# Turning the normalised x by a DMA transpose instead of on TensorE, in a gated cross-attention block

## The reference

```
x = x + tanh(g_xattn) * xattn(layernorm(x), ctx, ctx)      # 16 heads of 16
    q = layernorm(x) @ Wq.T + bq ; k = ctx @ Wk.T + bk ; v = ctx @ Wv.T + bv
    out = softmax(q k.T / 4) v @ Wo.T + bo
x = x + tanh(g_ffn) * ffn(layernorm(x))                    # 4-bit weights, 16-bit activations,
                                                           # a global maximum between the stages
```

## Time and profile before

| | |
|---|---|
| median of three runs | 587.03 us |
| the profiled execution's own time | 588.25 us |
| its span | 586.4 us |
| PE busy | 544.4 us (93%) |
| DVE busy | 483.0 us (82%) |
| ACT busy | 435.1 us (74%) |
| POOL busy | 191.8 us (33%) |

### The profile page before, as it was taken

How to read it: one execution, slowest core, us unless ns; L and a number is a source line. 1 busy time by engine, 2 the same in 40 slices (tenths; PEclk the granted TensorE clock), 3 DMA queues, 4 the chain that set the end, 5 groups by cost and what they waited for, 6 DMA issues and landing times. The chain is left out here.

```text
span 586.4 us, 12288 instructions
## 1 busy us (share of the span) xinstructions
PE 544.4 (93%) x4614; PEld 317.1 (54%) x4614; DVE 483.0 (82%) x818; ACT 435.1 (74%) x633; POOL 191.8 (33%) x298
## 2 busy tenths in 40 slices
PE   7779999999999998998787999999999899989998
PEld 2435555565556555664464544444444344458887
DVE  5687889999999999998556899979888799954532
ACT  2327888888888887887853454469999998889960
POOL 3412356776767697753551000000000000010000
PEclk9868999999999999999997999999999999999999
DMA  7322344546435453333220000000000000013443
GB/s 242 98 85 97 123 132 136 158 143 184 149 87 156 152 166 115 120 115 102 68 84 35 1 1 0 1 0 1 1 1 0 1 0 1 0 73 109 147 141 108
DMA packets 41472, 48.90 MB, mean 83 GB/s; under 512 B 9302, under 2 KB 29190, under 8 KB 41414
## 3 DMA queue, kind: packets, MB, share of 16 engines
q1 hardware_dynamic: 39430, 43.14, 23.6%
q0 software_dynamic: 1408, 4.46, 2.5%
q10 hardware_dynamic: 576, 0.52, 0.3%
HBM read 24.25 MB, written 8.63 MB: 56 GB/s over the span
## 5 line engine op out<-in xcount | busy, mean ns | idle before, releaser
L924 DVE TENSOR_REDUCE negm<-s_ps 128x2 bf16<-128x512 f32 x256 | 163.5, 684 | 16.6 <-PE s_ps L529 15.9
L732 ACT ACTIVATE pt<-st_ps 128x512 f32<-128x512 f32 x256 | 138.2, 594 | 40.6 <-PE st_ps L546 40.0
L1270 PE MATMUL pairs<-xq,wut 128*128 128x512 f16 x576 | 124.7, 379 | 2.7 <-ACT lnall L1464 1.6
L1270 PEld LDWEIGHTS pairs<-xq,wut 128*128 128x128 f16 x576 | 56.2, 98 | 71.1 <-issue 2.3
L529 PE MATMUL s_ps<-kst,qst 63*128 63x256 f16 x512 | 66.9, 282 | 16.6 <-DVE negm L924 13.7
L456 PE MATMUL pv_ps<-pt,vt 128*32 128x256 f32 x1024 | 68.5, 385 | 1.5 <-ACT ot L659 0.7
L1784 POOL PARTITION_ALL_REDUCE vmax<-vmax x5 | 1.8, 355 | 193.3 <-DVE vmax L1577 119.4
L1270 PE MATMUL pairs<-xq,wgt 128*128 128x512 f16 x276 | 60.5, 379 | 0.0
L546 PE MATMUL st_ps<-qst,kst 64*128 64x256 f16 x512 | 56.4, 272 | 1.7 <-ACT pt L732 1.7
L529 PEld LDWEIGHTS s_ps<-kst,qst 63*128 63x128 f16 x512 | 20.6, 94 | 54.7 <-DVE negm L924 39.7
L1376 PE MATMUL pairs<-wdt,h 128*128 128x256 f16 x384 | 47.2, 273 | 2.9 <-DVE h L1739 2.4
(11 more groups left out here) (229 smaller groups left out, 1036.7 us busy)
## 6 DMA issues: line engine op xcount, KB each, us to landing
qst<-qk SPq DMA_DIRECT2D x47, 128.0 KB, 2.1
kst<-qk SPq DMA_DIRECT2D x45, 128.0 KB, 2.1
xt<-in_x SPq DMA_DIRECT2D x16, 256.0 KB, 4.4
ct<-in_ctx SPq DMA_DIRECT2D x16, 256.0 KB, 2.9
xr<-in_x SPq DMA_DIRECT2D x16, 256.0 KB, 3.9
out<-y SPq DMA_DIRECT2D x16, 256.0 KB, 3.6
lnall<-out POOLq DMA_DIRECT2D x8, 512.0 KB, 4.3
recb<-rec_dram SPq DMA_DIRECT2D x15, 256.0 KB
```

The costliest lines, as they stand in the source:

```text
L732: nc.scalar.activation(pt[:, (j // 2) % 2, j % 2, :, r], st_ps[u % 3][:], ACT.Exp, scale=1.0 / (WS * WS * HD ** 0.5)).then_inc(exp_done, 1)
L924: nc.vector.tensor_reduce(negm[:, b % 2, :, lo], s_ps[r][:], AX.X, ALU.max, negate=True).then_inc(max_done, 1)
L1270: mm = nc.tensor.matmul(ps[:, p, k, :], w[:, a, dt, f * P:(f + 1) * P], xq[:, b, c, dt, :], start=n == 0, stop=n == len(terms) - 1)
```

## The change

For all batches but the first:

- the four transposes on TensorE (slot 6), ScalarE's copy of the bank and VectorE's subtraction (slot 7) are gone;
- ScalarE copies `xn` as it lies to f16 `xtok[:, 0]` at offset XH = -22 (slot 2), GpSimd subtracts and writes `xtok[:, 1]` at XL = -21 (slot 3);
- SyncE issues at XDMA = -19 (slot 5, between `stack_k` and `load_tops(b, 0)`) one DMA transpose of both halves, 256 KB, from `xtok` to `xtr`;
- the q projection (slot 1) waits for it (`x_turned`) and reads `xtr` in two runs of 128 columns;
- GpSimd's `normalise` waits for the copy and the subtraction of the last batch instead of TensorE;
- the two spare banks have six users, each with a fixed bank, and the waits are changed to match.

The first batch is still turned by TensorE, now in `st_ps[1]`.

```
+    XH, XL, XDMA = -22, -21, -19
-        xh = sb("xh", [P, 2, S], F16)
-        xl = sb("xl", [P, 2, S], F16)
+        xtok = sb("xtok", [P, 2, KT * D], F16)
+        xtr = sb("xtr", [P, 2, KT, 2, P], F16)
...
-            return misc[(7 * (g // PAIRS) + (0, 1, 1, 2, 3, 4, 5, 6)[g % PAIRS]) % 2]
+            return misc[{TOP1 % PAIRS: 0, Q % PAIRS: 1, K % PAIRS: 0, TOP0 % PAIRS: 1, V % PAIRS: 0, PROJ % PAIRS: 1}[g % PAIRS]]
...   # SyncE, behind stack_k and ahead of load_tops(b, 0)
+                if (b := batch(g, XDMA)) is not None and b:
+                    sp.wait_ge(xl_done, b + 1)
+                    sp.wait_ge(xh_done, b + 1)
+                    sp.wait_ge(q_done, b)
+                    sp.dma_start_transpose(xtr[:].rearrange("p i t u q -> p (i t u) q"),
+                                           xtok[:].rearrange("p i c -> p (i c)")).then_inc(x_turned, 16)
...   # TensorE, project_out
-                pe.wait_ge(v_taken, before(g, V))
-                pe.wait_ge(top_done[1], before(g, TOP1))
+                pe.wait_ge(top_done[0], before(g, TOP0))
...   # TensorE, Q
-                    pe.wait_ge(v_taken, before(g, V))
+                    pe.wait_ge(top_done[0], before(g, TOP0))
                     pe.wait_ge(xl_done, b + 1)
-                    project(bank(g), "q", xh, xl, q_done)
+                    if b:
+                        pe.wait_ge(x_turned, 16 * b)
+                    project(bank(g), "q", lambda k: xtr[:, 0, :, k, :], lambda k: xtr[:, 1, :, k, :], q_done)
...   # TensorE, TURN, now for the first batch alone
-                if (b := batch(g, TURN)) is not None:
-                    pe.wait_ge(top_done[0], before(g, TOP0))
-                    pe.wait_ge(ql_done, before(g, Q))
-                    pe.wait_ge(xl_done, b)
-                    pe.wait_ge(xn_ready, b + 1)
+                if g == TURN:
+                    pe.wait_ge(xn_ready, 1)
...   # ScalarE
-                if (b := batch(g, -17)) is not None:
-                    act.wait_ge(xt_done, b + 1)
-                    act.wait_ge(q_done, b)
-                    nc.scalar.copy(xh[:], bank(PAIRS * b + TURN)[:]).then_inc(xh_done, 1)
+                if (b := batch(g, XH)) is not None and b:
+                    act.wait_ge(xn_ready, b + 1)
+                    act.wait_ge(x_turned, 16 * (b - 1))
+                    nc.scalar.copy(xtok[:, 0], xn[:].rearrange("p t d -> p (t d)")).then_inc(xh_done, 1)
...   # VectorE
-                if (b := batch(g, -17)) is not None:
-                    dve.wait_ge(xh_done, b + 1)
-                    nc.vector.tensor_tensor(xl[:], bank(PAIRS * b + TURN)[:], xh[:], ALU.subtract).then_inc(xl_done, 1)
...   # GpSimd, normalise and behind it
-                    pool.wait_ge(xt_done, b)
+                    if b == 1:
+                        pool.wait_ge(xt_done, 1)
+                    else:
+                        pool.wait_ge(xh_done, b)
+                        pool.wait_ge(xl_done, b)
+                if (b := batch(g, XL)) is not None and b:
+                    pool.wait_ge(xh_done, b + 1)
+                    pool.wait_ge(x_turned, 16 * (b - 1))
+                    nc.gpsimd.tensor_tensor(xtok[:, 1], xn[:].rearrange("p t d -> p (t d)"), xtok[:, 0], ALU.subtract
+                                            ).then_inc(xl_done, 1)
```

More of the change, by code:

```diff
@@ L152, in attention, with two_halves @@
         recb_ps = s_ps[1][:].rearrange("p a b -> p (a b)")
-        last_ps = (misc[1][:, 0], st_ps[2][:, 0])
+        last_ps = (misc[0][:, 0], st_ps[2][:, 0])
         recx = wi[:, 0:4 * S].bitcast(F32)
-        ahl, all_ = (xh, ch), (xl, cl)
+        def two_halves(i):
+            return xtr[:, i].rearrange("p t u q -> p (t u q)").rearrange("p (u s) -> p u s", u=2)
+        ahl, all_ = (two_halves(0), ch[:]), (two_halves(1), cl[:])
         ident_zeroed = sem("ident_zeroed")
@@ L201, in attention @@
         xt_done = sem("xt_done")
+        x_turned = sem("x_turned")
         xh_done = sem("xh_done")
@@ L423, in project @@
                 for e in range(2):
-                    mm = split_product(to[:, e, :], lambda k: wh[nm][:, k, e * P:(e + 1) * P],
-                                       lambda k: wl[nm][:, k, e * P:(e + 1) * P],
-                                       lambda k: xh_[:, k, :], lambda k: xl_[:, k, :])
+                    o = to[:, e, :] if nm == "k" else to[:, e, :].rearrange("p (t q) -> p t q", t=KT)
+                    mm = split_product(o, lambda k: wh[nm][:, k, e * P:(e + 1) * P],
+                                       lambda k: wl[nm][:, k, e * P:(e + 1) * P], xh_, xl_)
                 mm.then_inc(done, 1)
@@ L514, in _ @@
             pe.wait_ge(cl_done, 1)
-            project(st_ps[0], "k", ch, cl, k_done)
+            project(st_ps[0], "k", lambda k: ch[:, k, :], lambda k: cl[:, k, :], k_done)
             spare_products(4)
@@ L576, in _ @@
                     pe.wait_ge(xl_done, b + 1)
-                    project(bank(g), "q", xh, xl, q_done)
+                    if b:
+                        pe.wait_ge(x_turned, 16 * b)
+                    project(bank(g), "q", lambda k: xtr[:, 0, :, k, :], lambda k: xtr[:, 1, :, k, :], q_done)
                 if (b := batch(g, K)) is not None and b:
                     pe.wait_ge(top_done[1], before(g, TOP1))
-                    pe.wait_ge(xl_done, before(g, TURN))
+                    pe.wait_ge(v_taken, before(g, V))
                     pe.wait_ge(kl_done, b)
                     pe.wait_ge(cl_done, b + 1)
-                    project(bank(g), "k", ch, cl, k_done)
+                    project(bank(g), "k", lambda k: ch[:, k, :], lambda k: cl[:, k, :], k_done)
                 if g == -6:
@@ L619, in _ @@
                 if (b := batch(g, TOP1)) is not None:
-                    pe.wait_ge(xl_done, before(g, TURN))
-                    pe.wait_ge(top_done[0], before(g, TOP0))
+                    pe.wait_ge(v_taken, before(g, V))
+                    pe.wait_ge(kl_done, before(g, K))
                     pe.wait_ge(max_done, UNITS * b + UNITS)
@@ L676, in high_last @@
                 act.wait_ge(v_done, NB)
-                nc.scalar.copy(ahl[v][:], at[:, 1 - v]).then_inc(ah_last, 1)
+                nc.scalar.copy(ahl[v], at[:, 1 - v]).then_inc(ah_last, 1)
             def high_of(b):
@@ L713, in _ @@
                     high(1, bank(PAIRS * b + K), kh_done)
-                if (b := batch(g, -17)) is not None:
-                    act.wait_ge(xt_done, b + 1)
-                    act.wait_ge(q_done, b)
-                    nc.scalar.copy(xh[:], bank(PAIRS * b + TURN)[:]).then_inc(xh_done, 1)
[L718 to L724, removed]
+                if g == TURN + 1:
+                    act.wait_ge(xt_done, 1)
+                    nc.scalar.copy(xtr[:, 0].rearrange("p t u q -> p u t q"),
+                                   st_ps[1][:].rearrange("p u (t q) -> p u t q", t=KT)).then_inc(xh_done, 1)
+                    act.wait_ge(kst_zeroed, 1)
+                    act.wait_ge(kl_done, 1)
+                    for d, i in enumerate((2, 3, 2)):
+                        act.dma_start(kst[d:P:4, 0].rearrange("p j q -> p (j q)"),
+                                      qk[:, i].rearrange("p h q -> p (h q)")).then_inc(stack_loaded[0], 16)
+                    weight_high("v", wv_loaded)
+                if (b := batch(g, XH)) is not None and b:
+                    act.wait_ge(xn_ready, b + 1)
+                    act.wait_ge(x_turned, 16 * (b - 1))
+                    nc.scalar.copy(xtok[:, 0], xn[:].rearrange("p t d -> p (t d)")).then_inc(xh_done, 1)
                 if 0 <= it < NB:
@@ L972, in _ @@
                     ln_max(LAST)
-                if (b := batch(g, -17)) is not None:
-                    dve.wait_ge(xh_done, b + 1)
-                    nc.vector.tensor_tensor(xl[:], bank(PAIRS * b + TURN)[:], xh[:], ALU.subtract).then_inc(xl_done, 1)
+                if g == TURN + 1:
+                    dve.wait_ge(xh_done, 1)
+                    nc.vector.tensor_tensor(xtr[:, 1].rearrange("p t u q -> p u t q"),
+                                            st_ps[1][:].rearrange("p u (t q) -> p u t q", t=KT),
+                                            xtr[:, 0].rearrange("p t u q -> p u t q"), ALU.subtract).then_inc(xl_done, 1)
                 if g == -16:
```

5 lines of the change are left out of this document (2 added, 3 removed).

## The result

The changed kernel takes 591.0 us (median of 16 runs, 587.05 to 595.7), the kernel before in the same job 587.85 (16 runs): ratio 1.0052, 95% interval 1.003 to 1.0073. It is slower by about 3 us; 583.9 was forecast.

The account below looks back on a forecast made before the run. Attention was taken to be bound by DVE and PE together, tied by the order within a round. From 587.03 us, -3.7 for the removed part and +0.6 for the start gave 583.9 us, range 580.5 to 593.

Parts of the forecast that it names:

- The removed part: Slots 6 and 7: taking transposes off PE and the subtraction off DVE wins 3.7 us over the steady part.
- The free subtraction: Slot 7 to slot 0: DVE's subtraction costs nothing, 1.95 us with or without it, since PE's output projection sets the time.
- both limits: Slot 0's reductions start no earlier than 2.54 us after slot 6's end, nor 1.58 us after slot 7's start.
- ACT and POOL: Added copy (slot 2) and subtraction (slot 3): cost taken as 0, POOL's 1.156 us a batch hidden by its idle time.
- The transpose's issue: SP's queue, slot 5: one DMA's issue, 0.45 to 0.67 us, with eight separate blocks (4.9 us) as the upper bound.
- D = 1.3: Delay in us that the transpose puts on `load_tops` in SP's queue; no stall expected below 1.5.
- what is queued behind it: `load_tops`: Slot 5: the nearer wait, st of slot 0 needing this 4 KB load, with about 1.5 us to spare.
- rival 2: SP's queue in slot 5: the transpose delays `load_tops`, making the kernel slower, 593.7 to 631.5 us; chance 0.20.
- 0.7 x 14: SP's queue: 9.8 us lost if the delay on `load_tops` were 2.2 us, 0.7 in each of 14 batches.
- That a wait costs what it shows: Stalls on `load_tops` priced at their own length: delay beyond 1.5 us, in each of 14 batches.
- The start: Batches 1 and 2: q's projection comes 0.9 us late, about 0.3 is given back, net +0.6 us.
- The range: Whole kernel: 580.5 to 593 us for 8 in 10, no change included.

Follow-up runs that it names:

- g1: Changed kernel with copy in slot 1, subtraction in slot 2, transpose issued in slot 4, first three batches turned on TensorE; 585.75 us, ratio 0.9965.
- e1: Changed kernel without the later batches' copy, subtraction and transpose, q reading batch 0's x throughout; 584.91 us, ratio 0.9949.
- f2: e1 with ACT's copy and POOL's subtraction put back, no DMA; 586.35 us, ratio 0.9971.
- e3: Changed kernel with the transpose issued behind `load_tops(b, 0)` instead of ahead of it; 591.81 us, ratio 1.0052.
- h4: g1 with the transpose issued again in slot 5, between `stack_k` and `load_tops(b, 0)`; 589.76 us, ratio 1.0019.
- h2: Changed kernel with two plain copies of 128 KB in place of the transpose, q from unturned x; 588.66 us, ratio 1.0016.
- h3: Changed kernel with one plain 256 KB copy in pieces of 256 B in place of the transpose, q from unturned x; 587.83 us, ratio 0.9989.
- f1: e1 plus a DMA transpose of a constant array at the same place of SP's queue, nobody waiting on it; 586.79 us, ratio 0.9986.
- e4: Changed kernel with batches 0 to 2 turned by TensorE and batches 3 to 15 by DMA; 591.72 us, ratio 1.0055.
- h1: g1 with only the first batch turned on TensorE instead of the first three; 588.6 us, ratio 1.0004.

## Why the prediction was wrong

- **The removed part: right.** 3.7 us forecast; slots 6 and 7 gave 2.2 in the profiled execution, and 3.2 without the round whose clock was low; in g1's trace, which has no such round, they gave 3.2, and e1 as a whole 3.0. The free subtraction and both limits stand.
- **ACT and POOL: taken as 0.** By themselves they may cost nothing (f2 against e1: 1.4 us by the medians, 0.2 by the means, within the noise). The argument, that POOL's idle time ahead of `al` covers the subtraction, left out DVE: beside the late queue the subtraction fell on DVE's clips, whose sum grew by 2.05 us.
- **The transpose's issue.** I argued for one issue of 0.45 to 0.67 and added 0.85 for the data, D = 1.3. The issue alone takes 1.29: the right number for the wrong reason, and near enough for `load_tops(b, 0)`, whose lead of 4.1 became 2.66 and which made st wait once in the whole kernel.
- **The step that failed: "what is queued behind it: `load_tops`".** I stopped at the first instruction behind the transpose. SP's queue has no gap from slot 5 to slot 1, so the 1.29 us go on to the second `load_tops`, whose data moreover come behind four transfers of 256 KB: of its lead of 5.79 (least 5.28) 4.69 (least 3.35) was left, where the waiting st products came 3.5 to 4.3 after the issue. They go on to `recb` as well, and by it to POOL and the clips. This is rival 2's mechanism with another victim, at a smaller price than that rival's 0.7 x 14. e3 shows that sparing the first victim alone gives nothing back, h4 against g1 that the place does, h2 and h3 that the issue's time makes the waits.
- **That a wait costs what it shows: wrong too.** Three us of waits stand against six of loss, and the clock makes up much of the rest. Rounds 1 to 14 of e1 take 3.2 us more than those of f2, which has e1's work and the split; e1's trace has two low stretches there, f2's none, so one costs an estimated 1.6 us. After's trace has three. Its sixteen executions say the same: two with a mean clock of 0.980 took 587.2 us on average, no more than before, three with 0.977 took 590.4, eight with 0.974 took 591.7, three with 0.971 took 594.3. One stretch more in a trace lowers its mean by 0.003. For the late stretch the traces show what preceded it, PE's wait behind the clips; for the early ones it stays open, as PE's waits in the ten us ahead of round 3 sum to 1.56 in e1, where the clock fell, and also in f1 and f2, where it didn't.
- **The start: +0.6 forecast, +0.3 at the start of round 2** (-0.30, +1.70 in round 0, -1.08 in round 1). q began at 25.61, not 25.1, behind a wait of 1.87 on the transpose. By e4, removing this wait alone brings nothing back.
- **The range** held the time, though the direction was the other one; the chance of 0.25 for slower should have been larger, since no row of a transpose was at hand and the queue that it joins had been read at one place only.

The Trainium skill, "Advanced Engine Details and Errata", section "X-Bar Transpose (TRN2)", says that transposing DMAs are as fast as plain ones. In this case's traces they aren't: 1.29 against 0.53 us of issue, 3.1 against 2.4 to landing for the same 256 KB. The Trainium skill, "VectorE: DVE Perf Modes", section "The three transpose paths", gives 1309 ns per block of 128x128; here eight blocks landed together in 3.1 us, so its figure can't be multiplied by the blocks.

## What to carry to other kernels

When a DMA is put into a queue, follow the queue behind it until the first gap, and compare for every later issue the lead that it has with what its landing needs, in its least round; the first victim needn't be the one that counts. Put a slow issue where the queue stands idle: the same transpose cost 3 to 4 us more in slot 5 (h4) than in slot 4 (g1). And when an instruction is moved to an earlier slot, check its order in the first rounds, where its input isn't there yet: in h1 everything that needs q waited for it. An engine with idle time isn't free either: ask what runs on the others while its new instruction does.

## What the runs showed of the hardware

- A DMA transpose of 256 KB within SBUF holds the issuing queue for 1.29 us (1.27 at the least, up to 2.18), one plain copy of the same data for 0.53, one in pieces of 256 B for 0.62, two copies of 128 KB for 1.18.
- Packets of 256 B did little by themselves: the plain copy in such pieces (57072 packets in all, against 43632 of the one in long ones) landed after 2.9 us instead of 2.4, with no wait on PE (h3).
- DVE's clip (128x512, int16 to f32) took 0.42 us with POOL idle and 1.4 to 2.45 beside POOL's 128x512 instructions (before, from 151.8 and 217.9).
- TensorE's granted clock fell to its lower level behind short waits, in f1 at 220.5 behind one of 1.34 us; a stretch at the lower level cost an estimated 1.6 us (e1 against f2).
- SP's issues are stretched now and then in every kernel: four `ot<-ot` took 2.50 us as a rule, but 3.75 at 110.53 in the kernel after, right ahead of its longest wait (120.89, 1.47 us). Such a delay is harmless as long as the lead holds it.

```profile
110.53 3.75 SPq L339 DMA_DIRECT2D ot<-ot  x4
116.55 0.57 SPq L328 DMA_DIRECT2D qst<-mrow  x1
```
